# Layer 0 of the next pass runs inside layers 1 and 2 of this one, and its depthwise convolution inside layer 3

## The reference

```
x = x + L0(gn(x))   # deformable sampling: a 3x3 convolution gives 2 offsets and a mask per pixel,
                    #   bilinear sample at the offset place, times sigmoid(mask);
                    #   then a depthwise 3x3 and a pointwise 128x128 convolution
x = x + L1(gn(x))   # 3x3 average pool; a 3x3 convolution gives 18 offsets and 9 masks per pixel;
                    #   9 bilinear samples per pixel, then a 3x3 convolution (deformable convolution)
x = x + L2(gn(x))   # 3x3 convolution, weights put together from w and r (sign terms)
x = x + L3(gn(x))   # pointwise product to two halves; horizontal and vertical strip attention with
                    #   tanh kernels of 5 taps; a spatial and a channel gate (sigmoid); pointwise product
```

## Time and profile before

| | us |
|---|---|
| median of 3 runs | 2032.02 (2031.22 to 2033.98) |
| the profiled execution, its own time | 2024.91 |
| its span, first to last instruction | 2023.0 |
| PE / DVE / ACT / POOL busy | 1685.6 / 1242.0 / 597.7 / 78.8 |
| granted clock of PE, mean | 0.911 of full speed |

### The profile page before, as it was taken

The page is one execution under the profiler, slowest core; times in us unless marked ns, Lnnn a source line. Parts: engine busy times, 40 slices in busy tenths (PEclk is TensorE's granted clock), DMA queues, the critical chain, the costliest instruction groups (busy, mean ns, idle before and its releaser), DMA issues.

```text
span 2023.0 us, 23653 instructions
## 1 busy us (share of the span) xinstructions
PE 1685.6 (83%) x7748; PEld 905.4 (45%) x7748; DVE 1242.0 (61%) x2281; ACT 597.7 (30%) x986; POOL 78.8 (4%) x92
## 2 busy tenths in 40 slices
PE   4979878898788987889878888879878798797984
PEld 3555344543445434554345533555335553355431
DVE  5655676546775387753877439664496654865546
ACT  2232422324324142230513305133141322313221
POOL 1000000000000000000001000010000000000000
PEclk8999989898889988899888998889989899897997
DMA  2000000000000000000000000000000000000000
GB/s 97 22 1 1 1 23 22 1 1 1 23 22 1 0 1 23 22 1 0 1 23 22 2 0 1 33 12 1 0 1 33 12 1 0 1 22 1 1 0 21
DMA packets 7108, 22.80 MB, mean 11 GB/s; under 512 B 1233, under 2 KB 1937, under 8 KB 6929
## 3 DMA queue, kind: packets, MB, share of 16 engines
q1 hardware_dynamic: 6928, 20.58, 2.8%
HBM read 12.19 MB, written 8.39 MB: 10 GB/s over the span
## 4 chain that ended last, share of the span: by engine, by line
issue 73%; DVE 12%; PE 11%; POOL 2%; ACT 1%; DVEq 0%; POOLq 0%
PE psO L456 2%; DVE GQt L1349 2%; PE psO L482 1%; DVE GTs L1338 1%; POOL gst L407 1%; DVE samp L1407 1%; DVE hf L1315 1%; DVE img L1183 1%; DVE hf L1320 1%; PE ps L466 1%; POOL strip L415 1%; PE psN L482 1%; ACT xn L823 1%; DVE hf L1327 1%; DVE pool_v L1179 1%
## 5 line engine op out<-in xcount | busy, mean ns | idle before, releaser
L482 PE MATMUL psO<-samp,w 128*128 128x512 f32 x576 | 259.4, 596 | 10.1 <-ACT samp L801 10.1
L580 PE MATMUL psN<-GQt,xq 64*128 64x144 f32 x2048 | 188.2, 334 | 89.6 <-DVE GQt L1349 71.8
L823 ACT ACTIVATE xn<-x,gst 128x1024 f32<-128x1024 f32 x48 | 60.2, 1254 | 536.8 <-DVE gst L1065 536.8
L580 PEld LDWEIGHTS psN<-GQt,xq 64*128 64x128 f32 x2048 | 161.3, 215 | 122.6 <-issue 57.5
L801 ACT ACTIVATE samp<-psN 128x576 f32<-128x576 f32 x256 | 155.9, 649 | 161.5 <-PE psN L580 161.2
L482 PEld LDWEIGHTS psO<-samp,w 128*128 128x128 f32 x576 | 105.0, 190 | 118.9 <-issue 118.9
L482 PE MATMUL psN<-xn,w 128*128 128x512 f32 x288 | 131.5, 605 | 0.0
L482 PE MATMUL psO<-xn,w 128*128 128x512 f32 x288 | 129.8, 603 | 0.0
L801 ACT ACTIVATE xq<-psN 128x512 f32<-128x512 f32 x144 | 81.6, 598 | 85.4 <-PE psN L551 80.0
L1338 DVE TENSOR_TENSOR GTs<-hf 128x576 f32<-128x576 f32 x128 | 104.1, 823 | 3.4
L801 ACT ACTIVATE G<-psN 120x256 f32<-120x256 f32 x128 | 49.1, 384 | 187.9 <-PE psN L526 186.8
(11 more groups left out here) (162 smaller groups left out, 2656.5 us busy)
## 6 DMA issues: line engine op xcount, KB each, us to landing
xin<-in_x SPq DMA_DIRECT2D x16, 512.0 KB, 3.4
out<-yout SPq DMA_DIRECT2D x16, 512.0 KB, 2.7
w<-in_w SPq DMA_DIRECT2D x2, 576.0 KB, 5.4
samp<-in_r SPq DMA_DIRECT2D x1, 576.0 KB, 6.7
tab<-in_tab SPq DMA_DIRECT2D x1, 494.0 KB, 5.0
kh_w<-in_kh SPq DMA_DIRECT2D x1, 320.0 KB, 5.8
kv_w<-in_kv SPq DMA_DIRECT2D x1, 320.0 KB, 5.9
woT<-in_woT SPq DMA_DIRECT2D x1, 256.0 KB, 6.5
```

The lines of the kernel that those rows point to most:

```text
L482: last = mm(dst[:, h, :], wgt[:, k, :], rhs(h, k), start=(k == 0), stop=(k == K9 - 1))
L580: last = mm(pair(u)[:, g, :].rearrange("p (k r c) -> p k r c", k=K9, c=SW)[:, :, :, cols], xQ[rows, t, a, e, :], w[rows, e, :, :, cols], s ...
L823: nc.scalar.activation(inner(xn[s]), src[:].rearrange("p (r c) -> p r c", c=W), ACT.Identity, bias=g[:, 20:21], scale=g[:, 19:20]).then_in ...
```

## The change

- **Layer 0 moves forward by part of a pass.** The norms get names in place of numbers (S0 and S1 for the next x, L1A, L1B, L2A, ... for layer and sample), in the order in which they now come: L1B, S0, S1, L2A, L2B, L3A, L3B, L1A.
- The next x is normalised during layer 1, into img instead of xn. Its offset convolutions, offsets and far count stand between the products of conv1 of sample 1; its hats stand on DVE between layer 1's two residual sums.
- A new `layer0` on PE, ACT and DVE (with the branch on the far flag) holds the second half of conv2 of sample 0 and all of conv2 of sample 1, with the tiles of `near0` between the products. Both samples of near0 write psO[0], both of conv2 psO[1], so each second one waits until the first has been taken out. The residual of layer 2 goes to yout.
- conv0 has all 18 products of a sample on PE (`w0` holds 9 taps, DW_TAPS is gone). Those of sample 0 are spread over the end of layer 2 and layer 3 (`fill`), those of sample 1 stand at the head of the next pass and between the steps of layer 1's offsets. Residual, norm L1A and pool of sample 0 come at the end of the pass; those of sample 1 stand in the near sampling of sample 0.
- Layer 3 makes its first kernels before the U, XC and MEAN products. `blocks` of sample 0 use psO[1] and stand in one row behind conv0.
- The first pass's layer 0 is done ahead of the loop, without anything in between. The last pass has no next x.

The core of the diff:

```diff
@@ PE, layer0(j, i): the near branch
+                        conv2(0, {(1, k): lambda k=k: near0(j, 0, k - 2) for k in range(2, K9)}, (1,))
+                        near0(j, 0, TILES - 1)
+                        pe.wait_ge(added.sem, added.at(i, 4))
+                        near0(j, 0, TILES)
+                        hooks = {(0, 2): third_mean}
+                        for n, hk in enumerate(((0, 3), (0, 5), (0, 7), (1, 0), (1, 2), (1, 4), (1, 6), (1, 8))):
+                            hooks[hk] = lambda n=n: near0(j, 1, n)
+                        conv2(1, hooks)          # waits for added 5 (first sum of layer 2) and xn of L2B
+                        near0(j, 1, TILES)
@@ PE, one_pass, the head of a pass
+                conv0(i, 1, 0, 7)
                 pe.wait_ge(y_ready.sem, y_ready.at(i, 0))
                 pe.wait_ge(pooled_ready.sem, pooled_ready.at(i, 1))
                 offset_parts(2, img[0], w1off)
+                conv0(i, 1, 7, 10)
                 offsets(i, 2, 27)
+                conv0(i, 1, 10, 12)
                 doubles(i, 0)
+                conv0(i, 1, 12, 14)
                 far(i, 2)
-                blocks(i, 0, range(2, TILES))
+                conv0(i, 1, 14, 18)
+                blocks(i, 0, range(TILES))
...
-                        near(i, s)
+                        near(i, s, lambda t, s=s: group_mean(i, "L1B", order) if s == 0 and t == 0 else None)
@@ PE, conv1 of sample 0, then of sample 1
+                            hooks[0, 1] = lambda: group_mean(i, "S0", order)
+                            hooks[0, 3] = lambda: group_mean(i, "S1", order)
...
+                            hooks[0, 2] = lambda: next_parts(0)
+                            hooks[0, 7] = lambda: next_parts(1)
+                            hooks[1, 0] = next_offsets
+                            hooks[1, 4] = lambda: offsets(i + 1, 1, 3)
+                            hooks[1, 8] = lambda: start_far(i + 1)
@@ PE, layer 2 and 3
+                conv(psO[1], w2, window(xn[0]), halves=(0,))
+                group_mean(i, "L2B", order)
+                if more:
+                    layer0(i + 1, i)
...
+                fill(0, 4)
+                group_mean(i, "L3B", order)
+                fill(4, 7)
...                                              # the first product of layer 3, L734 before
+                fill(7, 14)
+                kernels(0)
...                                              # U
+                fill(14, 16)
...                                              # XC
+                fill(16, 18)
...                                              # MEAN
+                kernels(1)
@@ ACT, one_pass
                     parts(i, 2 + s)
+                    if s and more:
+                        normalise(i, "S0", order)
+                    if s:
+                        blocks(i, s, range(4))
...                                              # masks
+                    blocks(i, s, range(4 * s, TILES))
...                                              # in the near sampling of sample 0, after copy u:
+                            if s == 0 and u == 5:
+                                normalise(i, "L1B", order)
...
+                if more:
+                    normalise(i, "S1", order)
+                    parts(i + 1, 0)
+                    wide(i + 1, 0, i, order)
+                normalise(i, "L2A", order)
+                if more:
+                    parts(i + 1, 1)
+                    wide(i + 1, 1, i, order)
+                    start_masks(i + 1)
+                normalise(i, "L2B", order)
+                if more:
+                    layer0(i + 1)
@@ DVE, one_pass: near sampling of sample 0 (part 0 ahead of its tiles, part 1 after n == 2, POOL_AT = 4 to 7)
+                    if part == 0:
+                        residual0(i, 1)
+                        stats(own, "L1B", order)
+                    elif part == 1:
+                        affine(own, "L1B", order)
                     else:
+                        pool3(own, 1, part - 2, i, order)
...                                              # behind it
+                    if s == 0 and more:
+                        for k in range(2):
+                            start_stats(own, i + 1, k, order)
+                        for k in range(2):
+                            affine(own, ("S0", "S1")[k], order)
                 for s in range(2):              # the residual sums of layer 1
+                    if s and more:
+                        start_offsets(own, i + 1)
+                        for k in range(2):
+                            start_hats(own, i + 1, k)
...
+                if more:
+                    layer0(own, i + 1, i)        # weights, block copies; residual2(i, 0), stats L3A between the samples
+                affine(own, "L3A", order)
+                residual2(i, 1)
+                stats(own, "L3B", order)
+                affine(own, "L3B", order)
@@ DVE, the end of layer 3
+                if more:
+                    residual0(i + 1, 0)
...                                              # csum
-                    start_hats(nxt, 0)
...                                              # the two gates
-                    start_hats(nxt, 1)
+                    stats(own, "L1A", order)
...                                              # output sums, affine L1A between them
+                    for part in range(4):
+                        pool3(own, 0, part, i, order)
```

More of the change, by code:

```diff
@@ L720, in one_pass, with fill @@
+                def fill(first, last):
+                    if more:
+                        conv0(i + 1, 0, first, last)
+                fill(0, 4)
+                group_mean(i, "L3B", order)
+                fill(4, 7)
+                pe.wait_ge(xn_ready.sem, xn_ready.at(i, nth("L3B", order)))
                 pe.wait_ge(added.sem, added.at(i, 6))
@@ L735, in one_pass, with half, kernels @@
                     last.then_inc(l3_product.sem, 1)
+                def half(m, h, lhsT, rhs):
+                    mm(product(m), lhsT, rhs[:, HALF * h:HALF * h + HALF], start=True, stop=True)\
+                        .then_inc(l3_product.sem, 1)
+                def kernels(v):
+                    for h in range(2):
+                        pe.wait_ge(l3_dw.sem, l3_dw.at(i, 2 * v + h + 1))
+                        for t in range(TAPS):
+                            half(p_kern(v, h) + t, h, (kh_w, kv_w)[v][:, t, :], dwo)
+                fill(7, 14)
+                kernels(0)
                 for h in range(2):
@@ L778, in one_pass @@
                     last.then_inc(l3_product.sem, 1)
-            start_means(0, True)
-            start_parts(0, 0)
-            start_parts(0, 1)
-            start_offsets(0)
+                    if more and s == 0:
+                        group_mean(i, "L1A", order)
+            for s in range(2):
+                group_mean(0, ("S0", "S1")[s], FIRST)
+            for s in range(2):
+                pe.wait_ge(xn_ready.sem, xn_ready.at(0, s + 1))
+                start_parts(0, s)
+            for s in range(2):
+                offsets(0, s, 3)
             start_far(0)
@@ L833, in parts, with wide @@
                 last.then_inc(parts_ready.sem, 1)
-            def start_normalise(j, first):
-                for s in range(2):
-                    normalise(j, block0_norm(s, first))
-            def start_parts(j, s):
-                act.wait_ge(xn_ready.sem, xn_ready.at(j, s + 1))
-                copy(strip12[s][:], wide_windows(xn[s][:])).then_inc(wide_ready.sem, 1)
-                parts(j, s)
+            def wide(j, s, i, order):
+                act.wait_ge(xn_ready.sem, xn_ready.at(i, nth(("S0", "S1")[s], order)))
+                copy(strip12[s][:], wide_windows(img[s][:])).then_inc(wide_ready.sem, 1)
             def blocks(i, s, tiles):
@@ L996, in one_pass @@
                 act.wait_ge(l3_csum.sem, l3_csum.at(i, 1))
                 nc.scalar.activation(st3[:, 2:3], st3[:, 1:2], ACT.Sigmoid, scale=1.0 / N).then_inc(l3_csig.sem, 1)
+                if more:
+                    normalise(i, "L1A", order)
             act.wait_ge(borders_zero, 8)
-            start_normalise(0, True)
-            start_parts(0, 0)
-            start_parts(0, 1)
+            for s in range(2):
+                normalise(0, ("S0", "S1")[s], FIRST)
+            for s in range(2):
+                wide(0, s, 0, FIRST)
+                parts(0, s)
@@ L1003, in _ @@
             start_masks(0)
+            layer0(0)
+            normalise(0, "L1A", FIRST)
             if PASSES > 1:
@@ L1229, in one_pass @@
-                for s in range(2):
-                    dve.wait_ge(conv_ready.sem, conv_ready.at(i, s + 1))
-                    v_.tensor_tensor(x[s][:], psO[s][:].rearrange("p b c -> p (b c)"), xin[s][:], ALU.add)\
-                        .then_inc(added.sem, 1)
-                    dve.wait_ge(added.sem, added.at(i, s + 1))
-                    stats(own, 2 + s, x[s])
```

(11 more changed lines are left out.)

596 lines of the change are left out of this document (309 added, 287 removed).

## The result

| | before | after |
|---|---|---|
| median, beside each other on one chip | 2033.00 (2031.22 to 2034.58, 4 runs) | 2063.32 (2061.84 to 2064.24, 4 runs) |
| ratio, 95% interval | | 1.0149 (1.0131 to 1.0166) |
| span of the profiled execution | 2023.0 | 2060.0 |
| granted clock of PE, mean | 0.911 | 0.923 |

What follows compares the result with a forecast made beforehand. PE was busy 83% yet not full, with layer 3 set by DVE. Stretches summed to +2.2 us a pass, 15.4 for seven; +4 prologue and +10.6 last pass made +30.0, 2055 profiled, 2062 with 7.1 more; 8-in-10 range 2026 to 2084.

Steps and rivals of the forecast that it cites:

- The likeliest case: Whole kernel: slower, at 2062 us, itself 2048 to 2076; chance 54%.
- C: Near sampling of sample 0: 18.1 us becomes 20.5, +2.4 a pass, bounds 0 and 4.
- A: Layer 3's output products to layer 1's offset convolution of sample 0: mean 54.4 us becomes 15.5, -38.9 a pass.
- G: Layer 3: mean 57.8 us becomes 54.0, -3.8 a pass, bounds -2.5 and -7.4; conv0 products in waits for DVE are free.
- The 7.1 that the forecast added: Whole kernel: median of three runs (2032.0) above the profiled execution (2024.9), added to 2055 to give 2062.
- B: Layer 1, offset convolution of sample 0 to its near sampling: 20.5 us becomes 27.1, +6.6 a pass.
- D: conv1 of sample 0: PE waits about 3 us for ACT's copy; +3.7 a pass, bounds 0.5 and 4.5.
- E: conv1 of sample 1: offset convolutions, offsets and a far count add in full, +13.3 us a pass, bounds 13 and 15.
- F: conv2 to layer 3's first product: near0's 16 tiles and waits add +18.9 us a pass, bounds 15.5 and 24.
- The rival with the clock: Filled PE, from layer 3 to the loop's turn, keeps its high clock: -6.9 us a pass, 2014 in all; 15%.
- The slower rival: Whole kernel: the interleaving costs more than the sum of its parts, slower than the forecast; 18%.
- The faster outcome: Whole kernel ends faster than before by more than 0.2% (4 us); chance 0.19.

Runs made afterwards that it cites:

- Run 3: Changed kernel with DVE's residual and statistics of sample 1 behind the first tile of near sampling instead of ahead of the tiles: 2053.77 us, ratio 1.0108.
- Run 2: Changed kernel with ACT normalising L1B after its fourth copy of near sampling instead of its sixth: 2041.04 us, ratio 1.0037.
- run 1: Changed kernel with ACT normalising S0 behind the four block copies in layer 1's second sample instead of ahead of them: 2043.14 us, ratio 1.0058.
- run 8: Changed kernel with 10 of conv0's 18 products of sample 0 left out inside layer 3: 2080.55 us, ratio 1.0239.
- runs 4: Changed kernel with DVE's affine L3A between near0's tiles of sample 1 instead of ahead of layer 2's last residual: 2061.79 us, ratio 1.0143.
- Run 11: Changed kernel with the order changes of runs 1 to 4 together, and the group mean of L3B behind two products instead of four: 1997.25 us, ratio 0.982.
- run 6: Kernel before, with layer 0's offset convolutions cut to 8 of 18 products: 2047.70 us, ratio 1.0089.
- 12: Kernel before, with ten products of each sample in layer 0's offset convolutions 128 columns wide instead of 512, instructions in place: 2052.69 us, ratio 1.0107.
- run 5: Changed kernel with layer 0's offset convolutions cut to 8 of 18 products: 2071.97 us, ratio 1.0199.
- run 9: Changed kernel with ten products of each sample in layer 0's offset convolutions 128 columns wide instead of 512, instructions in place: 2046.89 us, ratio 1.0056.
- run 7: Kernel before, with all nine taps of layer 0's depthwise convolution on PE and none on DVE: 2111.58 us, ratio 1.0401.

## Why the prediction was right, and where it was not

**The sum and its parts.** The likeliest case held: slower by 30 us against a forecast of +30, every stretch moved the way that was forecast, and only C lies outside the bounds given for it. What left A and G (43.8 us a pass) came back in the others, with 2.8 more. But the exactness is partly luck. The two spans differ by 37, not 30; of the 7 too many, 4.3 are in the passes (19.7 against 15.4), 2.1 in the last pass and end (12.7 against 10.6) and 0.6 ahead of the loop (4.6 against 4). And the profiled execution of before lay 8 us under the median of its kernel (2024.9 and 2033.0), that of after only 1.5. The 7.1 that the forecast added for that did not return, and the short sum made up for it. PE's busy time rose by 53 us, not by the 70 of its new products; that goes with a mean granted clock up from 0.911 to 0.923, which no run prices apart.

**A: right in size, with one term misread.** The sum put 1.9 us on PE for the turn of the loop, as 2.63 less the 0.71 of a branch; the bound of 0 was the right end (833.94 + 0.86 = 834.80). The rows of the last pass show why the 2.63 was no price of the turn: 1.3 of it was a wait for DVE's output sum, and the new order puts products in front of that wait. The pool of DVE, "just hidden" in the forecast, is what ends the stretch, by 0.27 us. The low clock took part of the gain back: two of seven passes have 15.5 (granted 0.89, the others 1.00), and there output products take up to 1.91 us for two, at 0.50, where 1.02 is usual.

**B: right.** +6.4, with a wait of 4.7 where 3 were given, since blocks and products ran sooner. Run 3 shows that of the DVE work ahead of near sampling only 1.0 us is on the path; the rest is held by the residual that frees the banks, which the prediction did not name as a limit.

**C: the step that was too small.** +2.4 forecast, +4.4 measured, above its upper bound of 4. The wait for the normalisation was put at 1.9 and is 2.81, and the mean of L1B, which stands behind PE's first tile, adds 1.51 that was not in the sum. Run 2 gives 3.3 of it back by one number.

**D: right in mechanism, short by 0.7.** The wait for ACT's copy is there (2.56 us, "about 3"), and run 1 removes the whole rise but 0.5 by putting ACT's work in another order. What the forecast lacked is the low level behind the wait: D has a granted clock of 0.95 in six passes, and of 1.00 in all passes of run 1.

**E, G: right.** 13.5 and -3.7. E is gapless (29.28 of 29.28 busy). For G run 8 corrects the reason: the products in the waits of layer 3 are worth more than nothing, since without them the stage is 1 to 2 us longer.

**F: 1.4 too high.** The waits came, but smaller: 0.77 for the mean of L2B (1.2 forecast), 0.62 at the branch (0.8, an estimate near the 0.71 of DVE at 593.14), and 0.96 for the shared accumulator (1.1), where the last block copy of sample 0 stands on DVE behind the first residual sum. For the first block PE waits nothing where 0.5 was put. A wait that the sum did not have is the 0.58 at 1015.99, for PE's own last sampling products at the end of the branch. Affine L3A on the end is not 1.3: runs 4 and 11 give 0.8 for it, and only together with the mean's place.

**The rival with the clock.** It fell in this change: four vertical kernels at 803.95 and the gates at 821.55 still take 3.78 us at a granted clock of 0.50, behind waits of 4.5 and 6.3 us, as the argument against it said; only the first product of layer 3 halved (3.68 us at 0.50 to 2.00 at 1.00). The output products were not at the low level in every pass of before: at 278.67 they take 1.02 to 1.12 us for two. As a cause it is real, though: in runs 6, 8 and 12 the stretches behind the emptier layer 3 are 1 to 5 us a pass longer, with a lower granted clock (A 0.89 instead of mostly 0.97 in 6 and 12, and mostly 0.84 to 0.89 instead of 1.00 in 8; D 0.93 or 0.94 instead of mostly 1.00 in five passes of 6 and of 12).

**The slower rival.** It had the interleaving cost more than its parts add up to. In the changed kernel F came out 1.4 under its forecast and the branch cost 0.62, under the 0.8 of the sum, so that rival fell. In run 5 the branch did come out dear, at 3.6 to 3.9 us: 3.69 in the pass shown with the code in another place, against 0.62 in run 9 with the code in the old one. What PE does in that time no run shows. The upper end of the range, 2084, which takes most of this rival in, was the author's estimate.

**The faster outcome** was given up too easily. Run 11 has layer 0 inside layers 1 and 2 as the changed kernel has, and is 1.8% faster than before. Two places in ACT's order, two in DVE's and one in PE's cost it 66 us (2063.3 - 1997.3). So in this case the move is a gain once the orders are right, and not before.

**Open.** Whether DVE's taps (80 us in the old order by run 7) would pay in the new one was not tried, nor whether such changes of order would have made the kernel before faster too. What makes the clock fall in one pass and not in the next of the same run, and so puts the runs of 1 and 9 in two groups, no run tells.

## What to carry to other kernels

When work is moved ahead of a wait, read the order of every other engine at the place where it lands: here a normalisation two copies too late and one ahead of four copies cost more (3.3 and 4.4 us a pass) than the whole change lost (2.8). Before a moved stage is judged, place each small producer (statistics, affine, normalisation) right behind its input and ahead of nothing that another engine needs sooner, and try these orders together: alone three of them gave 10 to 22 us and affine L3A 1.5, within its spread. The four together gave 54, the sum of what each gave alone, and with the group mean moved as well it was 66. And an experiment that leaves work out is no measure of that work's cost unless it keeps the instructions in place and PE busy: here it brought a branch of 3.69 for 0.62 us (run 5) and a layer 3 at a granted clock of 0.80 to 0.81 for 0.87 to 0.91 (run 8).

## What was not expected of the hardware

- The turn of the loop costs PE next to nothing: 2.63 us of issue there, but 2.40 at the entry of the last pass, which has no turn. DVE shows 2.62 us at the turn and none at that entry.
- One and the same branch cost 0.62 us or 3.6 to 3.9 us (runs 9 and 5); the place of the code is the one difference found ahead of it.
- Taking products off PE made both kernels slower (run 8: 70 products of 0.87 us less, +17 us; run 6: 5.3 us a pass less, by what it took in run 5, +16 us), and part of what follows ran at the low level. In run 8 four instructions behind a wait of 6.64 instead of 0.29 us took 3.78 instead of 1.98 us, and two output products behind an unchanged wait (2.29) took 2.07 instead of 1.12, each at a granted clock of 0.50 instead of 1.00.
- Issue ahead of an instruction can hide a wait: the 3.77 us in run 3 end 1.24 us after the residual sum that the branch waits for, and the 2.63 us before 1.3 us after the output sum.
